# First attention: encoder rows a batch ahead, low parts of the contexts on VectorE

## What is computed

```python
Sim = (enc @ w1)[:, :, None] + (ctx @ w2)[:, None, :] + einsum('id,jd->ij', enc * w3, ctx) + b
A = softmax(Sim, axis=2)
hq_hat = A @ ctx
Batt = softmax(max(Sim, axis=2), axis=1)
hc_bar = sum_i Batt[i] * enc[i]
x = x + concat([enc, hq_hat, enc * hq_hat, enc * hc_bar]) @ W_qv + b_qv
```

## Time and profile before

| | |
|---|---|
| time, median of 3 runs | 1044.96 us |
| lowest and highest run | 1043.93 to 1051.17 us |
| the profiled execution's own time | 1044.77 us |
| its span, first to last instruction | 1042.9 us |
| mean granted TensorE clock | 0.935 |
| busy: TensorE, VectorE, ScalarE, GpSimd | 895.4, 633.0, 510.3, 416.3 us |

### The profile page before, as it was taken

The page is one execution under the profiler, slowest core; times in us unless marked ns, Lnnn a source line. Parts: engine busy times, 40 slices in busy tenths (PEclk is TensorE's granted clock), DMA queues, the critical chain, the costliest instruction groups (busy, mean ns, idle before and its releaser), DMA issues. The chain is left out here.

```text
span 1042.9 us, 19551 instructions
## 1 busy us (share of the span) xinstructions
PE 895.4 (86%) x6158; PEld 792.0 (76%) x6159; DVE 633.0 (61%) x1408; ACT 510.3 (49%) x1098; POOL 416.3 (40%) x351
## 2 busy tenths in 40 slices
PE   4789799876999980489989999996769999999995
PEld 3678789764999980367878787775559999999995
DVE  6873735276555558478778778784844444444442
ACT  3542322153444440368678587574545555555552
POOL 2462422002555530527345254230034555555542
PEclk9998999968999995699999999999679999999998
DMA  9620100074676635401011010004946666666662
GB/s 300 211 81 11 32 1 1 2 257 137 215 236 222 233 132 166 143 2 41 22 41 41 1 41 2 1 27 146 339 152 192 203 202 200 199 201 199 200 189 28
DMA packets 68002, 131.58 MB, mean 126 GB/s; under 512 B 8000, under 2 KB 50624, under 8 KB 62816
## 3 DMA queue, kind: packets, MB, share of 16 engines
q1 hardware_dynamic: 55456, 110.27, 31.7%
q0 software_dynamic: 12480, 20.48, 7.9%
HBM read 109.08 MB, written 21.64 MB: 125 GB/s over the span
## 5 line engine op out<-in xcount | busy, mean ns | idle before, releaser
L1747 PEld LDWEIGHTS d_hps<-d_xg_t,d_xw 128*128 128x128 f32 x1248 | 150.3, 197 | 6.9 <-DVE d_xg_t L1929 5.5
L1747 PE MATMUL d_hps<-d_xg_t,d_xw 128*128 128x128 f32 x1248 | 150.8, 281 | 4.9 <-DVE d_xg_t L1929 4.9
L1656 ACT ACTIVATE x<-d_hps,b 128x128 f32<-128x128 f32 x312 | 88.9, 367 | 125.0 <-PE d_hps L1747 117.8
L826 POOL TENSOR_SCALAR c_prob<-c_prob,c_rinv 128x1024 f32<-128x1024 f32 x64 | 71.5, 1123 | 140.2 <-DVE c_rinv L1226 139.8
L1757 PE MATMUL d_yps<-d_w,d_hid_hi 128*128 x312 | 116.7, 406 | 2.3 <-DVE d_hid_lo L1938 2.3
L1582 POOL DMA_INDIRECT out_x<-d_y,d_take_slot x39 | 63.8, 1635 | 115.2 <-DMA out_x<-d_y,d_take_slot 89.5
L1233 DVE TENSOR_TENSOR c_pt_lo<-c_tp,c_pt_hi 128x512 fp32r<-128x512 f32 x128 | 82.1, 683 | 5.0 <-ACT c_pt_hi L1082 4.7
L1760 PE MATMUL d_yps<-d_w,d_hid_lo 128*128 x312 | 81.8, 283 | 0.0
L1219 DVE CUSTOM_DVE_ANT_0 c_prob<-c_sc,c_minf 128x1024 f32<-128x1024 f32 x64 | 75.6, 1219 | 8.3 <-PE c_sc L893 8.3
L1747 PEld LDWEIGHTS b_hps<-b_xg_t,b_w 128*128 128x128 f32 x624 | 76.1, 194 | 4.4 <-issue 2.2
L1747 PE MATMUL b_hps<-b_xg_t,b_w 128*128 128x128 f32 x624 | 77.7, 278 | 1.3 <-DVE b_xg_t L1926 0.7
(11 more groups left out here) (366 smaller groups left out, 2212.4 us busy)
## 6 DMA issues: line engine op xcount, KB each, us to landing
d_xw<-in_w SPq DMA_DIRECT2D x39, 1024.0 KB
b_w<-in_w SPq DMA_DIRECT2D x47, 512.0 KB, 7.5
d_w<-in_w SPq DMA_DIRECT2D x8, 1024.0 KB, 12.4
a_raw<-in_ctx_t SPq DMA_DIRECT2D x8, 512.0 KB, 5.7
a_raw<-in_ctx SPq DMA_DIRECT2D x8, 512.0 KB, 4.7
ybuf<-a_zero SPq DMA_DIRECT2D x2, 2048.0 KB
b_ysum<-ybuf SPq DMA_DIRECT2D x8, 512.0 KB, 7.6
c_ctx_t<-in_ctx_t SPq DMA_DIRECT2D x14, 256.0 KB, 3.1
```

The source lines that it names most:

```text
L826: nc.gpsimd.tensor_scalar(prob[w][:], prob[w][:], rinv[:, w:w + 1], 1.0, ALU.mult, ALU.mult).then_inc(s["prob_ready"], 1)
L1656: op = nc.scalar.activation(hid[q][:, h * FH + c, :], src[:, c, :], ACT.Gelu_apprx_tanh, bias=b1[:, ds(e, 1), h * FH + c])
L1747: mm = nc.tensor.matmul(hps[j % 2][h][:, c * P:(c + 1) * P], w1[j % WL][:, k, at:at + P], xg_t[j % 2][:, k, :], start=(k == 0), stop=(k == ...
```

## The change

The rows of x are prepared a batch earlier, in a third buffer `enc`. `turn_enc(b + 1)` moves from the end of a pass to the place behind `turn(p * TB + 3)` in it, and `make_u` and `u_low` to the place behind `invert(b, 0)`; the waits ahead of `project` go. `norm_enc(b + 2)` runs at the end of pass b, `norm_enc(2)` in the opening. The second half of u is formed by ScalarE. `turn_maximum` moves behind `scores(b, 1)`, and `turn(b * TB)` ahead of `spread_maximum`. All low pieces of the contexts are formed by VectorE: the natural context of batch b behind `invert(b, 0)` and u, the transposed context of batch b + 1 behind `invert(b, 1)`. `own_scores` is done for its own batch in two parts and uses `prod_t` as its scratch. GpSimd keeps `normal`, `add_bias` (now behind `normal(b, 3)`) and the product. The square root's table is loaded ahead of the first use. In the diff the buffers' index `% 2` of `enc`, which becomes `% 3`, is left out.

```diff
 attention0: tensors
-        enc = [sb(f"enc{q}", [P, TB, D]) for q in range(2)]
+        enc = [sb(f"enc{q}", [P, TB, D]) for q in range(3)]
...
-        dot = sb("dot", [P, D])
 TensorE
                 def turn_maximum(p):
 
                     pe.wait_ge(s["mrow_ready"], p + 1)
-                    if p < B - 1:
-                        pe.wait_ge(s["enc_t_ready"], (p + 2) * KD)
-                    if p:
+                    if p + 2 < B:
+                        pe.wait_ge(s["u_ready"], p + 3)
+                        pe.wait_ge(s["enc_t_ready"], (p + 3) * KD)
+                    elif p:
                         pe.wait_ge(s["x_ready"], p * 2)
...
                     turn(p * TB + 3)
-                    turn_maximum(p)
+                    if more:
+                        pe.wait_ge(s["enc_ready"], (b + 2) * TB)
+                        if p:
+                            pe.wait_ge(s["x_ready"], p * 2)
+                        else:
+                            pe.wait_ge(s["enc_t_ready"], 2 * KD)
+                        turn_enc(b + 1)
+                    if not now:
+                        turn_maximum(p)
                     values(p, 0, 1)
 
                     if now:
                         scores(b, 1)
+                        turn_maximum(p)
+                        turn(b * TB)
                     spread_maximum(p)
-                    if now:
-                        turn(b * TB)
                     values(p, 1, 0)
...
                         turn(b * TB + 2)
-                    if more:
-                        pe.wait_ge(s["enc_ready"], (b + 2) * TB)
-                        pe.wait_ge(s["hc_ready"], p + 1)
-                        turn_enc(b + 1)
-                    if now:
                         values(b, 0, 0)
-                    if more:
-                        pe.wait_ge(s["u_ready"], b * KD + 2 * KD)
-                        pe.wait_ge(s["enc_t_ready"], b * KD + 2 * KD)
                     project(p)
 ScalarE
-                def keep_enc(b, k, order):
-                    act.wait_ge(s["enc_tp"], b * KD + k + 1)
-                    if order:
-                        act.wait_ge(s["u_ready"], b * KD + k + 1)
+                def keep_enc(b, k):
                     nc.scalar.activation(enc_t[b % 3][:, k, :], ex[:, k * 512:(k + 1) * 512], ACT.Copy).then_inc(s["enc_t_ready"], 1)
 
                 def u_high(b):
-                    keep_enc(b, 1, False)
+                    act.wait_ge(s["enc_tp"], b * KD + 2)
+                    if b:
+                        act.wait_ge(s["u_lo"], b * KD)
+                    nc.scalar.activation(u_t[:, 1, :], ex[:, 512:1024], ACT.Identity, scale=wsim[:, 2 * KD + 1:2 * KD + 2],
+                                         bias=wsim[:, KD + 1:KD + 2]).then_inc(s["u_ready_a"], 1)
+                    act.wait_ge(s["u_ready"], b + 1)
+                    nc.scalar.activation(u_hi[b % 2][:, 0, :], u_t[:, 0, :], ACT.Copy).then_inc(s["u_hi"], 1)
+                    act.wait_ge(s["u_ready_a"], b + 1)
+                    nc.scalar.activation(u_hi[b % 2][:, 1, :], u_t[:, 1, :], ACT.Copy).then_inc(s["u_hi"], 1)
                     for k in range(KD):
-                        act.wait_ge(s["u_ready"], b * KD + k + 1)
-                        nc.scalar.activation(u_hi[b % 2][:, k, :], u_t[:, k, :], ACT.Copy).then_inc(s["u_hi"], 1)
-                    keep_enc(b, 0, True)
+                        keep_enc(b, 1 - k)
...
                 act.wait_ge(s["head_in"], 16)
+                nc.scalar.activation(m.spare1[:], m.const[:, C_EPS:C_EPS + 1], ACT.Sqrt)
                 root(FIRST, 6)
...
                     if now:
                         exponential(b, 0)
+                    if more:
+                        u_high(b + 1)
+                    if now:
                         split_high(2 * b + 1, cn_hi[b % 2])
...
                         exponential(b, 3)
-                    if more:
-                        u_high(b + 1)
 VectorE
                 def make_u(b):
 
-                    for k in range(KD):
-                        dve.wait_ge(s["enc_tp"], b * KD + k + 1)
-                        if k:
-                            dve.wait_ge(s["enc_t_ready"], b * KD + 1)
-                        nc.vector.tensor_scalar(u_t[:, k, :], ex[:, k * 512:(k + 1) * 512], wsim[:, 2 * KD + k:2 * KD + k + 1],
-                                                wsim[:, KD + k:KD + k + 1], ALU.mult, ALU.add).then_inc(s["u_ready"], 1)
+                    dve.wait_ge(s["enc_tp"], b * KD + 1)
+                    nc.vector.tensor_scalar(u_t[:, 0, :], ex[:, 0:512], wsim[:, 2 * KD:2 * KD + 1],
+                                            wsim[:, KD:KD + 1], ALU.mult, ALU.add).then_inc(s["u_ready"], 1)
...
+                def split_low(n, hi, lo, half):
+                    dve.wait_ge(s["raw_hi"], n * 2 + half + 1)
+                    nc.vector.tensor_tensor(parts_of(lo, half), raw_of(n, half), parts_of(hi, half),
+                                            ALU.subtract).then_inc(s["raw_lo"], 1)
...
                 norm_enc(0)
-                dve.wait_ge(s["raw_hi"], KD)
-                nc.vector.tensor_tensor(parts_of(ct_lo[0], 1), raw_of(0, 1), parts_of(ct_hi[0], 1),
-                                        ALU.subtract).then_inc(s["raw_lo_d"], 1)
+                split_low(0, ct_hi[0], ct_lo[0], 0)
                 dve.wait_ge(s["wsim_in"], 16)
                 make_u(0)
+                split_low(0, ct_hi[0], ct_lo[0], 1)
                 u_low(0)
...
                 maximum(0, 3)
+                for half in range(2):
+                    split_low(1, cn_hi[0], cn_lo[0], half)
                 low_parts(1)
                 invert(0, 3)
+                for half in range(2):
+                    split_low(2, ct_hi[1], ct_lo[1], half)
                 make_u(1)
                 u_low(1)
                 low_parts(2)
+                norm_enc(2)
                 dve.wait_ge(s["w_in"], 64)
-                own_scores(0)
+                own_scores(0, range(TB))
                 row_maximum(0)
-                own_scores(1)
...
                     if now:
                         invert(b, 0)
+                    if more:
+                        make_u(b + 1)
+                        u_low(b + 1)
+                    if now:
+                        for half in range(2):
+                            split_low(2 * b + 1, cn_hi[b % 2], cn_lo[b % 2], half)
+
+                    if now:
+                        maximum(b, 1)
                     dve.wait_ge(s["mrow_tp"], p + 1)
                     nc.vector.tensor_reduce(ngmax1[:], ex[0:1, 8:8 + P], AX.X, ALU.max, negate=True).then_inc(s["ngmax1_ready"], 1)
-
                     if now:
-                        maximum(b, 1)
+                        low_parts(b * TB)
                     dve.wait_ge(s["ngmax_bc"], p + 1)
                     nc.vector.tensor_copy(ngmax[:], ex[:, 136:137]).then_inc(s["ngmax_ready"], 1)
                     if now:
-                        low_parts(b * TB)
                         invert(b, 1)
-
+                        own_scores(b, (0, 1))
+                    if more:
+                        for half in range(2):
+                            split_low(2 * b + 2, ct_hi[1 - b % 2], ct_lo[1 - b % 2], half)
...
                     op.then_inc(s["wenc_ready"], 1)
-                    if more:
-                        norm_enc(b + 1)
+                    if now:
+                        own_scores(b, (2, 3))
                     dve.wait_ge(s["av_done"], p + 1)
                     nc.vector.tensor_copy(hq_t[:, 1, :], av[:, S:2 * S]).then_inc(s["hq_d"], 1)
-                    if more:
-                        own_scores(b + 1)
...
                         invert(b, 3)
-                    if more:
-                        make_u(b + 1)
-                        u_low(b + 1)
+                    if b + 2 < B:
+                        norm_enc(b + 2)
                     add_projection(p)
 GpSimd
-                def split_low(n, hi, lo):
-                    for half in range(2):
-                        split_low_half(n, hi, lo, half)
-
-                def split_low_half(n, hi, lo, half):
...
                     if now:
                         normal(b, 0)
-                        split_low(2 * b + 1, cn_hi[q], cn_lo[q])
                         normal(b, 1)
-                        if more:
-                            split_low(2 * b + 2, ct_hi[1 - q], ct_lo[1 - q])
                         normal(b, 2)
-                        add_bias(b)
...
                     if now:
                         normal(b, 3)
+                        add_bias(b)
```

(11 more changed lines are left out.)

25 lines of the change are left out of this document (11 added, 14 removed).

## The result

| | before | changed |
|---|---|---|
| median of the runs | 1045.02 us (4 runs) | 1032.51 us (4 runs, 1031.85 to 1033.93) |
| profiled execution, own time and span | 1044.77, 1042.9 | 1033.16, 1031.3 |
| mean granted clock | 0.935 | 0.941 |

The ratio is 0.9864 with an interval of 0.9832 to 0.9897: faster by 1.0 to 1.7%. The same program run again beside other kernels gave 0.9893 (0.9872 to 0.9913). The prediction was 1034.2 us in a range of 1030 to 1041.

The account below looks back on a forecast made before the run. TensorE was taken to bound a pass at 40.0 us of work, plus its waits and half clock. Start -2.4, pass 1 -3.05, pass 2 -5.6 and pass 3 +0.5 total -10.55, from 1044.77 to 1034.2 us; range 1030 to 1041.

Parts of the forecast that it names:

- The waits ahead of `project`: Passes 1 and 2 lose 5.45 and 5.44 us of TensorE wait and 2.4 us each of half clock.
- The opening: Up to turn(0): stats start 2.9 us earlier and a slow add loses 1.4 us, 4.3 us in sum.
- From there to batch 1: From turn(0) to the first scores of batch 1: start at 40.0 us, 2.4 us earlier than 42.38.
- The step with GpSimd held: End of batch 0: GpSimd and VectorE block each other, ending at 40.0 us; with GpSimd never held, 38.3.
- Pass 1: First loop pass: -5.45 and -2.4, plus a 3.1 us wait at spread_maximum and 1.7 of clock, -3.05 us.
- The clock term: Half clock behind the new spread_maximum waits: 1.7 us charged for pass 1, nothing for pass 2.
- a sign of being wrong: Prediction wrong if the spread_maximum wait exceeds 4 us, half clock behind it exceeds 3.4 us, or project still waits.
- rival (b): No new fall of the clock, or GpSimd not held: 1032.5 us, with both 1030.8; chance 0.24.
- (a): The forecast itself, with one fall of the clock: 1034.2 us, band 1032.7 to 1035.7; chance 0.40.
- Pass 2 and 3: Pass 2: -7.9 us plus a 2.3 us wait at spread_maximum, -5.6; pass 3: 0.5 us of wait, +0.5.
- rival (e): Slower than before: VectorE's 1024-element subtractions cost 2.39 us each, as GpSimd's did; 1047.7 us, chance 0.06.
- (d): project still waits, for hq_t and the product, now behind own_scores: 1041.3 us, or 1039 if less; chance 0.06.

Follow-up runs that it names:

- e2_low_pieces_only: The kernel before with only the low pieces moved to VectorE, encoder rows still prepared late; ratio 0.9976, median 1040.8 us.
- e9_rows_only: The changed kernel with all low pieces but one formed by GpSimd, as before the change, in the opening too; ratio 0.9868, median 1028.23 us.
- e7_bias_held: The changed kernel with add_bias(0) on GpSimd held until u_low(1) is done; ratio 0.9887, median 1029.44 us.
- e4_kept_warm: The changed kernel with ten needless matmuls just ahead of the first scores of batch 1; ratio 0.9901, median 1031.11 us.
- e8_all_together: The changed kernel with natural pieces behind invert(b, 1), add_bias(0) held, one opening piece on GpSimd, others spread, ngmax1 ahead of maximum(b, 1); ratio 0.9786, median 1018.2 us.
- c1_changed_again: The changed kernel run again with no edit, for a second profile; ratio 0.9893, median 1030.74 us.
- e6: The kernel before with add_bias(0) on GpSimd held until u_low(1) is done; ratio 0.9968.
- e3_maximum_first: The changed kernel with the two natural-context low pieces moved from ahead of maximum(b, 1) to behind invert(b, 1); ratio 0.9819, median 1023.0 us.
- e1_again: Second run of the changed kernel with the loop's low pieces back on GpSimd, opening unchanged; ratio 0.9823, median 1024.71 us.
- e10: The kernel of e8_all_together with the loop's low pieces on GpSimd; ratio 0.9762, median 1018.53 us.

## Why the prediction was right, and which terms were not

**The waits ahead of `project`.** As predicted: gone in passes 1 and 2, with the half clock behind them. e2_low_pieces_only keeps them and stays at 0.9976; e9_rows_only drops them and has the whole gain. This is shown.

**The opening.** `maximum(0, 0)` was put at 20.0 and came at 19.26. I had the stats wait for the rows of x until 14.4; they began at 13.73, when `u_low` ended, since the rows landed 10.4 us after their issue this time. The 1.6 us add went as said (0.18 now, and 2.19 in e9_rows_only, where GpSimd's pieces are back). `norm_enc(0)` fell from 3.41 to 1.38, but my reason was half of it: in e9_rows_only it took 1.38 too, for with the table loaded early it starts 1.3 us earlier and is done before GpSimd's piece begins. Of the 5.0 us, 3.66 are the pieces' move and 1.3 the rest.

**From there to batch 1.** Predicted 40.0, measured 38.72, of which 0.7 is the opening's. The step with GpSimd held was right, with its order wrong: I gave it the ports between pieces three and four (normal 33.8 to 34.9). It asked at 32.24 and got them at the end of both, so its 1.12 us took 2.96; piece four was not held, and `add_bias` began at 35.17 and held `u_low` to 2.95. The Trainium skill, page "SBUF — State Buffer", section "SBUF: two separate sides", says that whoever starts first keeps the pair for its whole instruction and the other blocks. The trace agrees in both directions here: GpSimd's normalisation took 2.96 us for 1.12, and VectorE's two `u_low` 2.95 beside `add_bias`, 1.29 without it in e7_bias_held. It shows one thing more: GpSimd asked during the first of VectorE's two pieces and was held through the second as well.

**Pass 1.** Predicted -3.05 with a wait of 3.1 us and 1.7 us of clock; the two profiles gave -6.03 (wait 2.35, no new fall) and -2.18 (wait 2.19, 6.83 us at half). The wait was 0.75 us oversized: `ngmax1` was ready at +15.2 instead of +15.7, and TensorE came at +13.0 instead of +12.6 (the prediction's own 11.35 and 1.4 make 12.75). The clock term is the one that fails. I sized it by the length of the wait, 2.4 us as harmless and 3.9 as costly. The two profiles have it the other way round, and a half clock of 6.83 us is twice what I allowed, which I had named as a sign of being wrong. The kernel before has two stretches of 6.83 us at half clock too, from 77.62 and from 125.41 us, around the ends of its 5.4 us waits, and I did not use them to size this term. In the first profile rival (b)'s "no new fall" held, in the second the clock cost more than (a) allows. The second's sum over attention 0, -10.38 us, is close to the -10.55 of the prediction only because its start was 0.75 us better than forecast and its pass 1 0.87 us worse.

**Pass 2 and 3.** Predicted waits 2.3 and 0.5, measured 2.18 and 0.61 us; passes -5.6 and +0.5, measured -5.80 and +0.71. ScalarE's Identity took 0.785 us at the median, a fifth of a us over the lower bound that I took, with no table load and free beside `make_u`. All pieces but one (1.62) took 1.20 to 1.22 us, so rival (e) had no ground. `project` waited for nothing in passes 1 to 3, so (d) had none either.

**What pass 1 is paced by.** The prediction had TensorE's start and VectorE's chain move together. The profiles of e4_kept_warm and e7_bias_held show that they needn't: TensorE gained 1.1 and 1.7 us there and stood most of it out, at `spread_maximum` and, in e7_bias_held, ahead of the next scores. A us at the start of pass 1 counts only as far as VectorE comes earlier too. Against the first profile `maximum(1, 0)` came 0.5 us earlier for 1.7 in e7_bias_held, and 2.2 us for 3.0 in e8_all_together (41.53 for 43.70). A long fall of the clock turns it round: in c1_changed_again this maximum came at 44.76, released by TensorE's scores.

**Behind attention 0.** I put nothing there, and the first profile shows +3.15 us. Of the table by stretch, the part from the end of attention 0 to the first large matmuls of the feed-forward layer and the part behind the second router; first the changed kernel, then the same program again:

```profile
188.31:237.93 49.62, 30.80 (x165) 22.80 (x164) 32.97 (x111) 19.66 (x29) 3.10 (x3) 0.72 0.53 173
...
754.82:1031.30 276.48, 261.60 (x1948) 247.91 (x1948) 126.83 (x274) 135.56 (x390) 138.80 (x114) 0.97 0.60 177
```
```profile
192.68:238.71 46.03, 28.73 (x164) 19.59 (x164) 33.12 (x111) 19.57 (x29) 3.16 (x4) 0.74 0.57 186
...
753.22:1027.10 273.88, 261.16 (x1948) 246.97 (x1948) 126.39 (x274) 135.22 (x390) 138.66 (x114) 0.97 0.61 179
```

All behind attention 0 is 842.99 and 834.42 us, for one program; the kernel before had 839.84. The code there is the same in all 14 profiles of this case, and they range from 832.9 to 843.0 us, the first profile of the changed kernel being the longest. The three with the rows of x late (before, e2, e6) have 839.8, 836.1 and 837.9. So nothing speaks against the zero, and what is seen is the spread of single executions, 10 us. What sets it stays open.

**The total.** That the time came so near is in part luck. The first profile gained 14.75 us in attention 0 for the 10.55 forecast and lost 3.15 behind it; the second gained 10.38, by two errors that cancelled, and 5.42 more behind it. By the medians the change gained 12.5 us, and 11.5 in the group of c1_changed_again. The measured 1032.51 us is what rival (b) gives (1032.5), just below the band of (a), 1032.7 to 1035.7. But (b)'s conditions are met in part only: no new fall came in one of two profiles, and GpSimd was held.

## What to carry to other kernels

When a helper's work is moved to a faster engine, what counts is not its duration but what waits behind it in that engine's queue: the same pieces cost 3.6 us on VectorE ahead of a maximum, and nothing that is seen either on GpSimd or on VectorE a few instructions later. After a wait is removed, look for the engine that then paces the stretch before removing the next one, since TensorE may only stand out what it gains (e4, e7). And read a second execution of the changed kernel before a difference of a few us in a stage is given a cause.

## What the runs showed that I had not expected

- The granted clock does not follow from the wait ahead alone. Behind waits of 2.35 and 2.18 us at `spread_maximum` it stayed at 1.00, behind one of 2.19 us at the same place of the same program it was 0.50 for 6.83 us, and in e3_maximum_first it fell at 170.75 for 3.41 us with no wait of over 1 us in that batch (e1_again, e8 and e10 fell in the same pass, at 170.29, 167.01 and 167.87). At the first scores of batch 1 a wait of 3.17 to 3.19 us went with 3.42 us at half clock in the first profile, 6.83 us in c1_changed_again and e2_low_pieces_only, and none in e1_again and e3_maximum_first. Why is open.
- A GpSimd instruction that asked while VectorE had two of its own in a row was held through both: 2.96 us for 1.12. In e7_bias_held it is 2.96 again.
- Identity out of PSUM with a scale and a bias per partition, 128x512, takes 0.785 us on ScalarE; two Copies of that size, one behind the other, took 1.07 together.
